# Row maxima of two heads in one VectorE instruction, in an attention kernel whose matmuls wait for them

## The reference

```
a  = gamma1(t) * rmsnorm(x) + beta1(t)
q, k, v = a Wq', a Wk', a Wv'              # 16 heads of 16 features each
x  = x + alpha1(t) * (softmax(0.25 * q k') v) Wo'     # per head, 512 x 512 scores
f  = gamma2(t) * rmsnorm(x) + beta2(t)
x  = x + alpha2(t) * ((silu(f Wg') * (f Wh')) Wout' + b)
y  = layernorm(x) * w + bias, shifted by tanh(t L' + l), then * w + bias again
```

## Time and profile before

| | us |
|---|---|
| median of three runs | 862.22 (860.38 to 864.31) |
| span of the profiled execution | 860.8 |
| PE busy | 778.7 (90%) |
| DVE busy | 577.5 (67%), of it `reduce_max` on `ps_m` 316.8 in 492 instructions |
| ACT busy | 489.5 (57%), of it the exponentials 247.4 in 256 |
| POOL busy | 171.2 (20%) |

### The profile page before, as it was taken

The page is one execution under the profiler, slowest core; times in us unless marked ns, Lnnn a source line. Parts: engine busy times, 40 slices in busy tenths (PEclk is TensorE's granted clock), DMA queues, the critical chain, the costliest instruction groups (busy, mean ns, idle before and its releaser), DMA issues. The chain is left out here.

```text
span 860.8 us, 14194 instructions
## 1 busy us (share of the span) xinstructions
PE 778.7 (90%) x4342; PEld 482.2 (56%) x4342; DVE 577.5 (67%) x1031; ACT 489.5 (57%) x791; POOL 171.2 (20%) x214
## 2 busy tenths in 40 slices
PE   2789989999999999999999989399499999999995
PEld 2434434444444444444445423289488888888884
DVE  1387687787787787787786863276765663765656
ACT  4328897676686686686686668354143342442432
POOL 2011021231321322223223213104801001011000
PEclk9859999999999999999999979799699999999998
DMA  5678564544645636536546451110000000000001
GB/s 168 209 248 315 176 206 157 181 161 161 210 134 177 218 99 220 183 119 205 173 150 206 149 186 42 58 53 20 0 26 1 26 1 24 24 0 25 26 1 49
DMA packets 59964, 103.02 MB, mean 120 GB/s; under 512 B 11857, under 2 KB 15593, under 8 KB 59801
## 3 DMA queue, kind: packets, MB, share of 16 engines
q1 hardware_dynamic: 42016, 84.58, 29.0%
q10 hardware_dynamic: 13688, 17.27, 6.3%
q0 software_dynamic: 4224, 0.73, 0.5%
HBM read 54.58 MB, written 39.07 MB: 109 GB/s over the span
## 5 line engine op out<-in xcount | busy, mean ns | idle before, releaser
L588 DVE TENSOR_REDUCE mx<-ps_m 128x1 f32<-128x512 f32 x492 | 316.8, 684 | 106.2 <-PE ps_m L749 93.0
L366 ACT ACTIVATE prob<-ps_s 128x1024 f32<-128x1024 f32 x256 | 247.4, 1020 | 63.6 <-PE ps_s L762 58.0
L749 PE MATMUL ps_m<-ks,qs 64*128 64x512 f32 x492 | 186.9, 479 | 8.5 <-DVE mx L588 3.3
L749 PEld LDWEIGHTS ps_m<-ks,qs 64*128 64x128 f32 x492 | 85.5, 190 | 148.8 <-DVE mx L588 135.9
L762 PE MATMUL ps_s<-qs,ks 64*128 64x512 f32 x512 | 134.6, 466 | 10.3 <-ACT prob L366 5.7
L776 PE MATMUL ps_o<-prob,v 128*32 128x512 f32 x1024 | 138.9, 614 | 3.8 <-ACT o_raw L382 3.1
L969 ACT ACTIVATE sil<-ps_g 128x512 f32<-128x512 f32 x64 | 38.3, 598 | 178.7 <-PE ps_g L1295 178.5
L260 POOL DMA_DIRECT2D qs<-m_hl x128 | 64.2, 508 | 232.1 <-DVE m_hl L563 227.4
L762 PEld LDWEIGHTS ps_s<-qs,ks 64*128 64x128 f32 x512 | 60.3, 188 | 46.6 <-ACT prob L366 18.2
L1312 PE MATMUL ps_f<-ow_hi,a_hi 128*128 128x256 f32 x256 | 73.0, 285 | 12.0 <-DVE raw L1085 11.1
L1312 PE MATMUL ps_f<-ow_lo,a_hi 128*128 128x256 f32 x256 | 73.0, 285 | 0.0
(11 more groups left out here) (174 smaller groups left out, 1342.3 us busy)
## 6 DMA issues: line engine op xcount, KB each, us to landing
stack_scratch<-qk_hi SPq DMA_DIRECT2D x64, 256.0 KB, 2.9
qs<-stack_scratch SPq DMA_DIRECT2D x32, 512.0 KB, 4.3
ks<-stack_scratch SPq DMA_DIRECT2D x32, 512.0 KB, 5.4
stack_scratch<-qk_lo SPq DMA_DIRECT2D x32, 256.0 KB, 3.3
v<-raw SPq DMA_DIRECT2D x32, 256.0 KB, 5.5
out_scratch<-o_raw ACTq DMA_DIRECT2D x30, 256.0 KB, 2.6
x_all<-in_x SPq DMA_DIRECT2D x8, 512.0 KB, 6.5
o_c<-out_scratch ACTq DMA_DIRECT2D x15, 256.0 KB
```

What stands on the lines that cost most here:

```text
L366: act.activation(prob[:, u % 2, 2 * h:2 * h + 2, :], ps_s[:, 2 * h:2 * h + 2, :], ACT.Exp, scale=SCALE).then_inc(p_r, 1)
L588: dve.tensor_reduce(mx[:, g % 2, i % 2, i // 2, qt:qt + 1], ps_m[:, i % 2, :] if bank is None else bank, AX.X, ALU.max)\
L749: pe.matmul(ps_m[:, i % 2, :] if bank is None else bank, qs[r:r + 64, g, j, qt * P:(qt + 1) * P], ks[r:r + 64, g, j, :], start=True, stop= ...
```

## The change

One VectorE instruction now takes the maxima of both heads of a pair: it reads both banks of `ps_m` (128 partitions, 2 x 512 values) and writes two values per partition. The first matmul of a pair waits for the reduction of the pair before, the second for nothing, and only the second raises `mx_full`. In `ORDER` M1 moves from behind S3 and S2 to behind M0.

```
-ORDER = ("S0", "S1", "M0", "S3", "S2", "M1", "A", "M2", "M3", "J")
+ORDER = ("S0", "S1", "M0", "M1", "S3", "S2", "A", "M2", "M3", "J")

         def max_bank(n):
-            n %= 2 + HG
-            return ps_m[:, n, :] if n < 2 else ps_s[:, n - 2, :]
+            n = n // 2 % 3
+            return ps_m[:] if n == 0 else ps_s[:, 2 * n - 2:2 * n]

-            def reduce_max(b, g, qt, i, free, bank=None):
-                n = UNITS * HG // NG * (NG * b + g) + HG * qt + i
+            def reduce_max(b, g, qt, j, free, banks=None):
+                n = HG // 2 * (TT * (NG * b + g) + qt) + j
                 dve.wait_ge(mx_full, n + 1)
                 if free is not None:
                     dve.wait_ge(job_full, free + 1)
-                dve.tensor_reduce(mx[:, g % 2, i % 2, i // 2, qt:qt + 1], ps_m[:, i % 2, :] if bank is None else bank, AX.X, ALU.max)\
+                dve.tensor_reduce(mx[:, g % 2, :, j, qt], ps_m[:] if banks is None else banks, AX.X, ALU.max)\
                    .then_inc(mx_red, 1)
...
-                    before = BEFORE.get(op, 2)
+                    before = BEFORE.get(op, 1)
...
-            def max_scores(b, g, qt, i, bank=None):
-                n = UNITS * (NG * b + g) + HG * qt + i
+            def max_scores(b, g, qt, i, banks=None):
+                j, r = i // 2, 64 * (i % 2)
+                n = HG // 2 * (TT * (NG * b + g) + qt) + j
                 if qt == 0 and i == 0:
                     pe.wait_ge(stack_in[g], 32 * (b + 1))
-                if bank is None:
-                    pe.wait_ge(mx_red, n - 1)
-                elif n >= 2 + HG:
-                    pe.wait_ge(mx_red, n - 1 - HG)
-                j, r = i // 2, 64 * (i % 2)
-                pe.matmul(ps_m[:, i % 2, :] if bank is None else bank, qs[r:r + 64, g, j, qt * P:(qt + 1) * P], ks[r:r + 64, g, j, :],
-                          start=True, stop=True).then_inc(mx_full, 1)
+                if i % 2 == 0 and banks is None:
+                    pe.wait_ge(mx_red, n)
+                elif i % 2 == 0 and n >= 3:
+                    pe.wait_ge(mx_red, n - 2)
+                out = ps_m if banks is None else banks
+                mm = pe.matmul(out[:, i % 2, :], qs[r:r + 64, g, j, qt * P:(qt + 1) * P], ks[r:r + 64, g, j, :],
+                               start=True, stop=True)
+                if i % 2 == 1:
+                    mm.then_inc(mx_full, 1)
```

More of the change, by code:

```diff
@@ L598, in _ @@
             dve.tensor_scalar(ss1[:, TT:2 * TT], ss1[:, TT:2 * TT], EPS_RMS, None, ALU.add).then_inc(ms1, 1)
-            for n in range(2 * UNITS):
-                reduce_max(0, n // UNITS, n % UNITS // HG, n % HG, None, max_bank(n))
+            for n in range(1, 2 * UNITS, 2):
+                reduce_max(0, n // UNITS, n % UNITS // HG, n % HG // 2, None, max_bank(n))
                 if n == UNITS - 1 + AHEAD:
@@ L612, in batch, with reductions @@
                     live = not (last and u >= UNITS // 2)
-                    def reductions(heads):
-                        for i in heads if live else ():
+                    def reductions(pairs):
+                        for j in pairs if live else ():
                             if u // TT < 2:
@@ L619, in reductions @@
                                 free = job_no(b, first, last, "MT2" if u // TT == 2 else "MT3")
-                            reduce_max(gb, g, qt, i, free if (qt == 0 and i == 0) else None)
+                            reduce_max(gb, g, qt, j, free if (qt == 0 and j == 0) else None)
                     op = jobs.get(u - 1)
-                    before = BEFORE.get(op, 2)
+                    before = BEFORE.get(op, 1)
                     reductions(range(before))
@@ L634, in batch @@
                             ffn_low(0, no)
-                    reductions(range(before, HG))
+                    reductions(range(before, HG // 2))
                     op = jobs.get(u)
@@ L734, in max_transpose @@
                 job_wait(no)
-                pe.wait_ge(mx_red, UNITS * (NG * b + g + 1))
+                pe.wait_ge(mx_red, UNITS // 2 * (NG * b + g + 1))
                 pe.transpose(ps_j[0:2 * HG * 2, 0:P], mx[:, g % 2].rearrange("p s j t -> p (s j t)"), ident[:])\
                   .then_inc(job_full, 1)
-            def max_scores(b, g, qt, i, bank=None):
-                n = UNITS * (NG * b + g) + HG * qt + i
+            def max_scores(b, g, qt, i, banks=None):
+                j, r = i // 2, 64 * (i % 2)
+                n = HG // 2 * (TT * (NG * b + g) + qt) + j
                 if qt == 0 and i == 0:
                     pe.wait_ge(stack_in[g], 32 * (b + 1))
-                if bank is None:
-                    pe.wait_ge(mx_red, n - 1)
-                elif n >= 2 + HG:
-                    pe.wait_ge(mx_red, n - 1 - HG)
-                j, r = i // 2, 64 * (i % 2)
-                pe.matmul(ps_m[:, i % 2, :] if bank is None else bank, qs[r:r + 64, g, j, qt * P:(qt + 1) * P], ks[r:r + 64, g, j, :],
-                          start=True, stop=True).then_inc(mx_full, 1)
+                if i % 2 == 0 and banks is None:
[7 more added lines that the diff above has]
+                    mm.then_inc(mx_full, 1)
             def scores(b, g, kb, i, fresh):
@@ L820, in _ @@
                     max_transpose(0, 0, PRO.index("MT0"))
-            pe.wait_ge(mx_red, 2 * UNITS - 2)
+            pe.wait_ge(mx_red, UNITS - 1)
             def batch(b, first, last):
```

## The result

| | before | after |
|---|---|---|
| median of the runs | 863.26 (860.38 to 867.18) | 881.79 (881.33 to 882.50) |
| span of the profiled execution | 860.8 | 880.7 |
| PE busy | 778.7 | 739.2 |
| DVE busy | 577.5 | 567.4 |

A forecast was written before the change was run, and what follows sets the result against it. The bound was taken to be the latency of a PE-DVE loop. Middle batches +10.6, first batch +2.5, last batch +1.3 and prologue -1.2 gave +13.2 us, 860.8 to 874.0 profiled, 875.4 median; range 866 to 889.

The forecast's parts named there:

- The loop: PE and DVE wait for each other; one turn of matmul pair, reduction and signal becomes 1.81 us, two in series per unit.
- the light unit: From one `attend` to the next, in unit 8 of a middle batch: 3.30 us becomes 3.62, the least time of any unit.
- Units 12 + 13: Middle batch, where `max_low` and the reciprocal stand between reductions: +0.58 us on 6.81.
- The first batch: Light units, units 5 and 13 and heavy units changed, the rest held by ACT or a lower clock: +2.5 us.
- Rival 3: A dearer reduction, through the second bank or second output: 1.37 us each, 25 us on top, 900 us; 7%.
- Units 0 to 3: Start of a middle batch, 14.84 us with ACT busy for 13.76: new least time 14.93, +0.1 us.
- Units 6 to 11: Middle batch: five heavy units, with a projection, 0.08 us shorter each (-0.40), light unit 8 longer by 0.32.
- Last batch: Maxima in its first 8 units only; three light ones go from 9.90 to 10.86 us, one more alike: +1.3 us.
- Prologue: 31 reductions without a gap become 16 pairs at 1.14 in place of 1.22 us: -1.2 us.
- DVE's throughput: Rival: DVE's work sets the time, so 246 x 0.08 = 20 us go away, about 842 us; 6%.
- Hidden anyway: Rival: the light units' 0.32 us vanishes behind ACT's exponentials, leaving +1, 863 us; 12%.
- The clock: Rival: a PE gap of about 0.9 us in light units lowers the matmul clock, 24 us on top, 898; 5%.

The follow-up runs named there:

- n_low_last: Changed kernel with VectorE's `n_low` in unit 2 moved from between the two merged reductions to behind both: 878.11 us, ratio 1.0172.
- pool_later: Changed kernel with GpSimd's `on_lo` issued later, behind the transfers of unit 5, VectorE's stream untouched: 878.72 us, ratio 1.0181.
- repaired: Changed kernel with `n_low` behind both reductions and VectorE's `job_full` wait of units 4, 8 and 12 moved one unit ahead: 875.39 us, ratio 1.0143.
- read_late_after: Changed kernel with the last batch's reads of the previous output, and what waits for them, one unit later: 883.69 us, ratio 1.0225.
- before: The kernel before the change, with separate reductions and the old order, unedited: median 863.26 us.
- read_late_before: Kernel before the change with the last batch's reads of the previous output, and what waits for them, one unit later: 862.3 us, ratio 0.9985.

## Why the prediction was right, and where its sizes were off

**The loop.** Right, and shown. The turn is 1.82 against 1.81, the light unit 3.65 against 3.62, M2 and M3 at A + 1.16 or 1.17, and units 5, 14 and 15 within 0.04. Three lengths of reduction obey one rule. Two more terms came out for partly wrong reasons, which is luck. Units 12 + 13 took 7.40 against 7.39 with 0.09 of the second wait in them, which the forecast hadn't; with that wait moved they take 7.30. The first batch is +2.6 against +2.5: the units named in the sum were right together (+2.5), while units 1 and 15, counted as unchanged, went by +0.53 and -0.58 and cancelled. One number of the prediction is wrong, and its sum doesn't use it: 125.1 to 491.6 us are 95 units and not six batches of 16, so a batch took 61.6 and not 61.1.

The Trainium skill, in "Perfetto Trace Analysis", section "Optimizing Scalar/DVE Operations", had said that smaller instructions may serve better on an engine that isn't saturated, and here the trace agrees: DVE waited 34 us more while it worked less. The estimate of 31 us of DVE time from that page's 125 ns does not come out: the reductions' busy time fell by 15.7 us, 64 ns for each of the 246 instructions saved.

**The instruction.** 1224 ns against 1.22 from a row of the same size on another operand. Rival 3 falls.

**Units 0 to 3, +1.36 against +0.10.** The failed step is "the light ones' loss goes into what ACT costs there anyway": I took the least time for the real one, with no unit above it. Of the 1.27 missed (16.20 against 14.93), 0.94 is unit 2 (4.56 against 3.62), `n_low` behind GpSimd, shown from two sides; 0.13 is unit 0, where the second wait stayed in every run, so that its part isn't shown; 0.17 is unit 3, 4.24 against 4.07, which I didn't follow further; 0.03 is unit 1. The prediction moved every start on DVE by tenths and never asked what an instruction of another engine does beside it.

**Units 6 to 11, +0.06 against -0.08, and unit 4.** The five heavy ones lost 0.38 of the 0.40 (unit 6 went from 4.20 to 4.10, unit 7 from 4.15 to 4.09). What the sum lacked is the second wait of units 4 and 8, 0.09 each, shown, and 0.03 of the light unit.

**Last batch, -3.3 against +1.3.** The failed step is "three light ones take 9.90 us and will take 10.86". That was right for these three (10.94); what I left out is that the gap and the slow units behind it in the earlier trace rows are a matter of where one transfer lands among ScalarE's instructions, and that a change of the pace moves it. The two rows were used for a rival and not for the sum.

**Prologue, +1.4 against -1.2.** The reductions did come 1.13 to 1.14 apart. But the failed step is that their time was taken as the time of the end: the squares of the next batch's input came later, and a matmul waited longer for ScalarE. PE's timeline there, before:

```profile
40.30 0.80 PE L749 MATMUL ps_s<-ks,qs 64*128 64x512 f32 x2 [0.61 <-ACT o_c L461]
```

and after, with DVE's ahead of it:

```profile
38.81 0.17 DVE L598 TENSOR_SCALAR ss<-ss 128x4 f32<-128x4 f32 x1 [7.31 <-ACT junk L315]
```

```profile
41.43 0.79 PE L750 MATMUL ps_s<-ks,qs 64*128 64x512 f32 x2 [2.17 <-ACT o_c L461]
```

L598 came 1.14 us later than before (at 37.67), and L461 behind it. That lateness can't be put down to the change: four more kernels have this very prologue (`n_low_last`, `pool_later`, `repaired`, `read_late_after`), and in their profiles L598 starts anywhere from 36.99 to 38.53 and the prologue takes 63.4 to 64.7 us. The mean of the five is 64.4, that of the two profiles with the old prologue and the old order (`before`, `read_late_before`) 64.1. So most of the +1.4 is the spread from one execution to the next, and what stands is that no saving of 1.2 shows.

**The rivals.** DVE's throughput (842) falls: it works 15.7 us less and waits 34 more. Hidden anyway (863) falls, as the light units grew by 0.35. The clock (898) falls for this change: over the 389 us of the middle batches the granted clock is 1.00, with PE idle for up to 1.09 at a time in the light units. It isn't nothing for kernels of this kind, though. Of the eight other kernels that wait by pairs, seven have a stretch at 0.50 somewhere in the middle batches of their profile, mostly a single one of 3.4 us, which costs 1.1 to 2.3 us; the three with separate waits have none there.

The errors of +2.6 in the prologue, +9 in the middle batches and -4.6 in the last one partly cancel, so the total is nearer than its terms, and that is luck.

## What to carry to other kernels

Where two engines hand a buffer to and fro, work out the turn (write, read, signal) and how many turns run side by side before merging instructions: the merged one here saved 0.06 us of each pair and gave up a second bank in flight, 0.35 us per light unit. A merged instruction with four banks, so that one pair fills while the other is read, would be the next thing to try; it wasn't tried here. What was tried is the order in which both inputs come together: without it the loss was nearly three times as large. When a change shifts one engine's starts, look at what other engines run at that moment, since an instruction can become 2.5 times as long by starting 0.13 us behind another.

## What the runs showed of the hardware

- A reduction of fp32 values from PSUM took 684 ns for 512 in one bank, and over two banks 692 for 512, 958 for 768 and 1224 for 1024; two of 512 in a row start 0.61 apart, so following another saves 0.07 of 0.68 and merging two saves 0.06 of 1.29.
- An instruction of DVE with two SBUF inputs took 1.69 us instead of 0.68 behind a GpSimd operation of 1.27 that had started 0.13 earlier; in the other order GpSimd's took 1.42 instead of 1.27 to 1.29.
- A second counter to wait for, directly ahead of a reduction, cost DVE 0.09 us in the last five of the middle batches, which are one loop in the program. In the one ahead of them, a loop of a single pass, it cost nothing that shows (M2 at A + 1.16), and moving it one unit ahead cost 0.07.
- A granted clock of 0.50 for 3.4 us came in kernels in which PE had stood still for less than 0.7 us at a time, three times within the 5 us before (0.38, 0.54 and 0.69 in `n_low_last`); the changed kernel, with gaps of up to 1.09, kept 1.00 over its middle batches. What decides between the two isn't shown.
